# Ranks ahead of the last window groups, VectorE's tables spread over eight expert tiles, and twelve first sums ahead of the tail

## The reference

```python
x = x + gnn(layernorm(x))     # 3125 nodes x 256; 53125 edges, 8 edge types, summed at dst
h = layernorm(x)
probs = softmax(h @ gate_w + gate_b)         # 16 experts
top_probs, top_idx = top_k(probs, 2)         # weights normalised over the two
hidden = silu(h @ w1[e]) * (h @ w2[e])       # 256 -> 512
x = x + sum_k top_probs[k] * (hidden @ w3[top_idx[k]])   # 512 -> 256
```

## Time and profile before

| | |
|---|---|
| median of 3 runs | 917.49 us (916.19 to 918.03) |
| the profiled execution | 918.04 us |
| its span, first to last instruction | 916.3 us |
| TensorE matmuls | 738.9 us busy, 81% |
| TensorE weight loads | 627.0 us, 68% |
| VectorE | 517.8 us, 57% |
| GpSimd | 658.9 us, 72% |
| ScalarE | 301.6 us, 33% |

### The profile page before, as it was taken

One profiled execution on the slowest core, in us unless ns is written; L12 is line 12 of the kernel. 1 busy time (PEld: TensorE's weight loads), 2 busy tenths in 40 slices (PEclk: granted clock), 3 DMA queues, 4 the chain that ended last, 5 costly groups with the idle time before them and its releaser, 6 DMA issues.

```text
span 916.3 us, 18023 instructions
## 1 busy us (share of the span) xinstructions
PE 738.9 (81%) x4626; PEld 627.0 (68%) x4627; DVE 517.8 (57%) x1444; ACT 301.6 (33%) x469; POOL 658.9 (72%) x614
## 2 busy tenths in 40 slices
PE   0136887989788898888888888779999999999980
PEld 0124676877667776677767676558888888888870
DVE  6887646365464545647445577884444444344448
ACT  5524225222343323324233333122333333233323
POOL 7777777777777777777777750259798786987772
PEclk9997889899899999979999898999999999999995
DMA  9873445454455333343334324066656655663546
GB/s 204 252 227 98 145 145 181 133 161 145 145 150 157 106 104 106 104 131 103 106 104 133 103 82 166 24 234 232 217 189 217 224 182 174 222 212 97 160 137 182
DMA packets 91488, 141.92 MB, mean 155 GB/s; under 512 B 13197, under 2 KB 65889, under 8 KB 91456
## 3 DMA queue, kind: packets, MB, share of 16 engines
q0 software_dynamic: 25680, 70.16, 26.4%
q1 hardware_dynamic: 48854, 56.28, 19.3%
q10 hardware_dynamic: 16922, 15.15, 5.2%
HBM read 108.61 MB, written 32.93 MB: 154 GB/s over the span
## 4 chain that ended last, share of the span: by engine, by line
PE 43%; POOL 23%; issue 16%; DVE 9%; DMA 7%; ACT 1%; DVEq 1%; POOLq 0%; ACTq 0%; SPq 0%
POOL got L575 21%; PE ps L1710 16%; PE ps L1692 9%; PE ps L1549 7%; PE ps L1561 6%; DMA got<-x_tab,gidx 5%; PE ps L1718 3%; PE ps L1676 1%; PE ps L1645 1%; DVE ps L1474 1%; POOL part L581 1%; DVE stat L995 1%; DMA part<-in_x,early_idx 1%; DMA y_tab<-ffn 1%; POOL part L609 0%
## 5 line engine op out<-in xcount | busy, mean ns | idle before, releaser
L575 POOL DMA_INDIRECT got<-x_tab,gidx x388 | 370.3, 954 | 119.5 <-issue 112.7
L1549 PE MATMUL ps<-hot,got 125*128 125x256 f16 x1700 | 222.9, 293 | 75.6 <-DMA got<-x_tab,gidx 66.1
L1549 PEld LDWEIGHTS ps<-hot,got 125*128 125x128 f16 x1700 | 173.0, 104 | 121.0 <-DMA got<-x_tab,gidx 40.0
L1120 DVE TENSOR_TENSOR store<-store,ps 128x512 f32 x150 | 102.6, 684 | 182.1 <-PE ps L1549 151.0
L1561 PE MATMUL ps<-part,store 128*128 128x256 f32 x800 | 184.3, 389 | 0.5 <-DVE acc L1131 0.5
L1710 PE MATMUL ps<-part,operands 128*128 x696 | 177.9, 404 | 4.2 <-DVE operands L1396 3.1
L1561 PEld LDWEIGHTS ps<-part,store 128*128 128x128 f32 x800 | 154.5, 196 | 21.2 <-issue 0.5
L1710 PEld LDWEIGHTS ps<-part,operands 128*128 128x128 f32 x696 | 127.5, 190 | 31.5 <-issue 5.0
L1102 DVE TENSOR_SCALAR hot<-key_row,pass,drel 125x256 f16<-125x256 f16 x425 | 125.8, 363 | 12.4 <-issue 7.4
L1692 PE MATMUL ps<-part,operands 128*128 x696 | 98.3, 290 | 3.0 <-DVE operands L1406 2.6
L609 POOL TENSOR_TENSOR part<-store,part 128x2048 fp32r<-128x2048 f32 (+1 forms) x28 | 98.0, 3501 | 2.3
(11 more groups left out here) (252 smaller groups left out, 682.4 us busy)
## 6 DMA issues: line engine op xcount, KB each, us to landing
store<-in_L_ffn_w SPq DMA_DIRECT2D x48, 512.0 KB, 4.8
y_tab<-ffn SPq DMA_DIRECT2D x9, 896.0 KB, 4.6
y_tab<-ffn ACTq DMA_DIRECT2D x58, 128.0 KB
xs_tab<-x_sb SPq DMA_DIRECT2D x14, 512.0 KB, 3.1
ffn<-xs_tab ACTq DMA_DIRECT2D x55, 128.0 KB, 2.2
got<-x_tab,gidx POOLq DMA_INDIRECT x388, 2.7
acc<-in_x SPq DMA_DIRECT2D x5, 560.0 KB
x_tab<-got SPq DMA_DIRECT2D x5, 560.0 KB
```

Of the source, the lines that this page charges most:

```text
L575: nc.gpsimd.indirect_dma_start(got[:, c, :], None, x_tab, bass.IndirectOffsetOnAxis(ap=gidx[:, col:col + 1], axis=0)).then_inc(gathered[g] ...
L1120: v.tensor_tensor(window, window, ps[:, WIN_BANK[g], :].rearrange("p (q n) -> p q n", n=WIN), ALU.add).then_inc(win_added, 1)
L1549: last = mm(ps[:, WIN_BANK[g], k * KEYS:(k + 1) * KEYS], got[0:CE, c, a * DIM + k * P:a * DIM + (k + 1) * P], hot[0:CE, g % HOT, c - c0, : ...
```

## The change

Three edits. TensorE's `ranks` call, with its two waits, moves ahead of groups 3, 4 and 5 of the last tile. VectorE's tables are cut up and their order is changed: the rank sum and one product come before the first `low_xs`, `positions` comes before `order_tables`, `oct_tables` comes after tile 1, the splits of the first two experts are moved by a place, and `slots_needed` and `result_weights` are divided over tiles 3 to 7. In the tail a bank now takes two tiles in one copy of 512 columns, so that 12 tiles have room; six copies and eleven first additions are placed in and after the last two expert tiles, ahead of the last `copy_y`, and the twelfth behind it.

```diff
+        SUMS = 2 * len(SUM_BANK)
+        SOON_SUMS = 3
+        def sum_at(t):
+            n = t % SUMS
+            return ps[0:TP, SUM_BANK[n // 2], n % 2 * DIM:(n % 2 + 1) * DIM]
...
+            def keep_sums(q):
+                t0, t1 = 2 * q, min(2 * q + 2, TILES)
+                if t0 >= SUMS:
+                    act.wait_ge(out_ready, t0 - SUMS + 2)
+                bank = ps[0:TP, SUM_BANK[q % len(SUM_BANK)], 0:(t1 - t0) * DIM].rearrange("p (t d) -> p t d", d=DIM)
+                nc.scalar.copy(bank, acc[:, t0:t1, :]).then_inc(first_sum, 1)
...
-            for u in range(2):
-                expert_tile(early + (LAST_PAIRS - 1), u, load=False)
+            keep_sums(0)
+            keep_sums(1)
+            expert_tile(early + (LAST_PAIRS - 1), 0, load=False)
+            keep_sums(2)
+            expert_tile(early + (LAST_PAIRS - 1), 1, load=False)
             act.wait_ge(y_done, final_j + 1)
             high_hid(final_j)
             store_y(final_j - 1)
+            act.wait_ge(hid_ready, final_j + 1)
+            act.sem_inc(tiles_begun, 1)
+            act.wait_ge(xsT_ready, final_j + 2)
+            act.sem_inc(tiles_begun, 1)
+            for q in range(3, 6):
+                keep_sums(q)
             store_y(final_j)
...
             for t in range(TILES):
                 act.wait_ge(out_ready, t + 1)
-                if t + banks < TILES:
-                    keep_sum(t + banks)
+                if t % 2 and t - 1 + SUMS < TILES:
+                    keep_sums((t - 1 + SUMS) // 2)
                 act.dma_start(out[t * TP + p0:t * TP + p1, :], acc[p0:p1, t, :]).then_inc(out_stored, 16)
...
             final_j = dve.value_load(final[0:1, 0:1], min_val=0, max_val=SLOT_TILES - 1)
+            step(v.tensor_reduce(rank[:, :], smaller[0:1, :, :], AX.X, ALU.add))
+            offset_hots(hot1)
             low_xs(0)
+            offset_hots(hot2)
+            positions()
             order_tables()
-            positions()
-            split_first(0, (DOWN_PART,))
...
-            expert_tile(0, 0, first=True, tables=oct_tables)
-            split_first(1, (UP_PARTS, DOWN_PART))
-            expert_tile(0, 1, tables=slots_needed)
-            result_weights()
+            expert_tile(0, 0, first=True)
+            split_first(0, (DOWN_PART,))
+            expert_tile(0, 1, tables=lambda: split_first(1, (UP_PARTS, DOWN_PART)))
+            oct_tables()
             expert_tile(1, 0)
-            expert_tile(1, 1)
-            expert_tile(2, 0)
-            expert_tile(2, 1)
+            expert_tile(1, 1, tables=lambda: rows_upto(0))
+            expert_tile(2, 0, tables=lambda: rows_upto(1))
+            expert_tile(2, 1, tables=slots_needed)
+            expert_tile(3, 0, tables=result_weights)
+            expert_tile(3, 1, tables=sorted_weights)
...
+            for u in range(2):
+                expert_tile(early + (LAST_PAIRS - 1), u, firsts=range(u * SOON_SUMS, (u + 1) * SOON_SUMS))
...
             low_hid(final_j)
+            for t in range(2 * SOON_SUMS, SUMS - 1):
+                add_first(t)
             copy_y(final_j)
-            ahead = len(SUM_BANK) - 2
-            for t in range(ahead):
-                add_first(t)
+            add_first(SUMS - 1)
+            ahead = SUMS - 4
             for t in range(TILES):
-                if t + ahead < TILES:
+                if SUMS <= t + ahead < TILES:
                     add_first(t + ahead)
                 add_second(t)
...
                     t = TILES - 1
+                    pe.wait_ge(choice_step, (b * GEN_W + w) * SWEEP_STEPS + 2 * CHOICE_STEPS)
+                    pe.wait_ge(win_added, (v0 + TILES) * NG + RANK_BANK + 1)
+                    ranks(0, FIRST_PART).then_inc(ranks_begun, 1)
                     window(v0, t, 3)
                     window(v0, t, 4)
                     window(v0, t, 5, sweep, ODD)
-                    pe.wait_ge(choice_step, (b * GEN_W + w) * SWEEP_STEPS + 2 * CHOICE_STEPS)
-                    pe.wait_ge(win_added, (v0 + TILES) * NG + RANK_BANK + 1)
-                    ranks(0, FIRST_PART).then_inc(ranks_begun, 1)
                     turn_x2(v0 + t - 2)
```

More of the change, by code:

```diff
@@ L1355, in _, with offset_hots @@
             dve.wait_ge(owner_done, 3)
+            def offset_hots(hot_k):
+                step(v.tensor_tensor(hot_k, hot_k, bc(t_off[:, :], TE, 1), ALU.mult))
             def positions():
-                for hot_k in (hot1, hot2):
-                    step(v.tensor_tensor(hot_k, hot_k, bc(t_off[:, :], TE, 1), ALU.mult))
                 for k, hot_k in enumerate((hot1, hot2)):
@@ L1407, in low_hid, with expert_tile @@
                                 hidT[:, 0, :, :].bitcast(F32), ALU.subtract).then_inc(hidT_ready, 1)
-            def expert_tile(i, u, first=False, tables=None):
+            def expert_tile(i, u, first=False, firsts=(), tables=None):
                 j = i * 2 + u
@@ L1412, in expert_tile @@
                     low_hid(j - 1)
+                    for t in firsts:
+                        add_first(t)
                     if tables:
@@ L1425, in _, with rows_upto @@
             final_j = dve.value_load(final[0:1, 0:1], min_val=0, max_val=SLOT_TILES - 1)
-            pairs = dve.value_load(pairs_i[0:1, 0:1], min_val=EXPERTS // 2, max_val=SLOT_TILES // 2)
+            early = dve.value_load(early_i[0:1, 0:1], min_val=EXPERTS // 2 - LAST_PAIRS, max_val=SLOT_TILES // 2 - LAST_PAIRS)
+            step(v.tensor_reduce(rank[:, :], smaller[0:1, :, :], AX.X, ALU.add))
+            offset_hots(hot1)
             low_xs(0)
+            offset_hots(hot2)
+            positions()
             order_tables()
-            positions()
-            split_first(0, (DOWN_PART,))
+            def rows_upto(k):
+                dve.wait_ge(upto_kept, 2)
+                step(v.tensor_tensor(mine, upto_tile, bc(same[:, EXPERTS - 2 + k, :], [1, TILES, EXPERTS], 1), ALU.mult))
+                step(v.tensor_reduce(upto[:, k, :], mine, AX.X, ALU.add))
             def slots_needed():
[L1434 to L1438, removed]
                 step(v.tensor_scalar(upto_i[:, :, :], upto[:, :, :], float(P - 1), None, ALU.add))
@@ L1459, in result_weights @@
                 v.tensor_copy(pos2[0:TP, :, :], low_hi[:, :, :]).then_inc(pos2_done, 1)
-            expert_tile(0, 0, first=True, tables=oct_tables)
-            split_first(1, (UP_PARTS, DOWN_PART))
-            expert_tile(0, 1, tables=slots_needed)
-            result_weights()
+            expert_tile(0, 0, first=True)
+            split_first(0, (DOWN_PART,))
+            expert_tile(0, 1, tables=lambda: split_first(1, (UP_PARTS, DOWN_PART)))
+            oct_tables()
             expert_tile(1, 0)
-            expert_tile(1, 1)
-            expert_tile(2, 0)
-            expert_tile(2, 1)
+            expert_tile(1, 1, tables=lambda: rows_upto(0))
[3 more added lines that the diff above has]
+            expert_tile(3, 1, tables=sorted_weights)
             def add_first(t):
                 dve.wait_ge(y_got[t], 16)
[L1472 to L1477, removed]
+                dve.wait_ge(first_sum, t // 2 + 1)
+                v.scalar_tensor_tensor(out=sum_at(t), in0=y1[0:TP, t, :], scalar=wts2[:, 0, t:t + 1],
+                                       in1=sum_at(t), op0=ALU.mult, op1=ALU.add).then_inc(part_done, 1)
+            with dve.Fori(4, early + (LAST_PAIRS - 1)) as i:
                 for u in range(2):
                     expert_tile(i, u)
+            for u in range(2):
+                expert_tile(early + (LAST_PAIRS - 1), u, firsts=range(u * SOON_SUMS, (u + 1) * SOON_SUMS))
             def add_second(t):
```

14 lines of the change are left out of this document (3 added, 11 removed).

## The result

| | before | after |
|---|---|---|
| median | 917.49 us (916.19 to 919.60, 5 runs) | 921.72 us (920.29 to 925.78, 5 runs) |
| ratio | | 1.0059 [1.0038, 1.0080] |
| the profiled execution, its span | 918.04, 916.3 | 925.78, 924.1 |

The change made the kernel slower by 0.59%, about 5 us (3.5 to 7.3); 911.0 was forecast, with 908.4 to 913.8 as range.

What follows compares the result with a forecast made beforehand. No engine was taken to bound the whole (TensorE 43%), so each edit was priced in its own stretch: -1.85 + 0.4 - 5.5 = -6.95 from 918.04 gives 911.1, taken as 911.0 us; range 908.4 to 913.8.

Steps and rivals of the forecast that it cites:

- Edit 1: Last tile's window groups: ranks moved ahead of group 3 fill TensorE's idle time, hiding their whole 1.85 us; -1.85 us.
- The step in which groups 4 and 5 still start by their gather near 543.9: Ranks end at 541.75, group 3 starts 0.3 late and ends near 543.2, before the gather at 543.91.
- Edit 3: Tail: 12 first additions go ahead, 38 remain; VectorE ends 5.9 us earlier, SyncE's stores give back 0.4; -5.5 us.
- Edit 2: Tables, 590 to 630 us: VectorE gives back over 5 us, but tile 6 waits for GpSimd's weight split; +0.4 us.
- Each lies in the gap of 1.49 us in which VectorE waits for TensorE: nothing on the path: Tiles 3 to 7: table pieces of 1.2 us or under 1.5 us fit VectorE's wait for TensorE and cost nothing.
- the meeting: Tables: VectorE's split from 598.4 meets the fourth GpSimd gather with 1.95 us left, 0.6 more than before.
- First, ScalarE loads tile 4's rows in order: ScalarE's load stays at 607.86, so tile 1's down matmuls start at 610.3, tile 3 near 612.5, tile 6 ready near 627.2.
- rival D: Slower: new TensorE idle stretches lower the granted clock, which stays low; at 5 tiles the end is 921; chance 0.03.
- the gate: Start of tile 6, held by GpSimd's split of the third expert's weights; its end goes from 629.29 to 630.2.
- A: Tile 6's wait for GpSimd also shortens, the oct's stores landing 2 us sooner; tables give -2: 908.6; chance 0.12.
- B: Tail bound by DMA well below the burst rate: -4.2 or less instead of -5.5, 912.3 to 914; chance 0.12.

Runs made afterwards that it cites:

- e15_scalar_tiles: Kernel before plus surplus tensor_scalar operations of 1 x 50, five in tile 4 and five in tile 5: 925.05 us, ratio 1.0084.
- e16_reduce_tiles: Kernel before plus surplus tensor_reduce operations on 1 x 50, five in tile 4 and five in tile 5: 917.86 us, ratio 1.0003.
- e13_all_soon: Changed kernel with the tables of tiles 3 to 7 moved right behind oct_tables, ahead of GpSimd's first split: 912.53 us, ratio 0.9943 to the kernel before.
- e14_ranks_and_sums: Changed kernel without the tables' new order and places, keeping early ranks and early sums: 911.09 us, ratio 0.9927 to the kernel before.

## Why the prediction was wrong

**Edit 1 (-1.85): right in sign.** Measured -2.8 us, from -1.3 to -4.2. The step in which groups 4 and 5 still start by their gather near 543.9 did not hold. The ranks ended at 541.36, sooner than the forecast 541.75 although the choice was 1.70 late in this execution, but group 3 began only at 543.75, behind the stand of 2.39 us, and then ran 1.25 us longer at the lower clock. Neither was in the forecast, and VectorE's add for tile 23 came at 556.19, not near 553.6. From choice to transpose the stretch is 1.0 us shorter where 1.85 was forecast, and less than the median shows; where the rest of the 2.8 comes from isn't settled.

**Edit 3 (-5.5): right.** Alone it gave -5.1 (-3.4 to -6.8). VectorE's last result came 15.65 us after `copy_y`, forecast 15.2; SyncE's last issue 1.15 us behind it, forecast 1.5 (its last nine issues took 4.25 us, 0.47 each instead of 0.54). The two errors cancel: 5.36 less in this stretch.

**Edit 2 (+0.4): wrong by 11 us when alone, and the cause of the miss.** The step that failed is "Each lies in the gap of 1.49 us in which VectorE waits for TensorE: nothing on the path", with the pieces of tiles 5 to 7 "at an estimated 0.2 each". The 0.18 is true only while GpSimd runs no split. The rows for the right price were there: the earlier trace rows has a GpSimd subtraction of 4.61 us over tile 5. I used the meeting in one direction only, VectorE's long split that holds up a GpSimd gather, and never asked what GpSimd's split does to VectorE's short work. The pieces had been moved into tiles where GpSimd splits; before, the short ones ran from 606.7 to 611.8 us, while it stood idle (its last gather ended at 606.00, its index copy came at 611.95). `e15_scalar_tiles` shows the price without any other edit: +7.7 us; `e16_reduce_tiles`, 0.

The operations on VectorE that read a PSUM bank (`low_hid`, `hid`, `low_xs`, `copy_y`) took their usual 0.42 and 0.69 beside the same splits, which is why the trace of before gave no hint in its durations. The Trainium skill (SBUF — State Buffer, "Who interferes with whom") has this as a rule: a `tensor_scalar` in a 2-port mode, or a `tensor_tensor` with both inputs in SBUF beside a GpSimd operation that reads SBUF, excludes the other for the whole instruction, whoever issued first goes first, and a `tensor_reduce` never contends on trn2. The traces agree in all three: 3.70 and 4.36 us for a `tensor_scalar` of 0.18, 2.11 for the `tensor_tensor` L1476 (0.19 without a split), 0.18 to 0.19 for the reduction. In which mode a `tensor_scalar` ran, no row shows.

A second step failed beside it, in the paragraph that begins "First, ScalarE loads tile 4's rows in order": it kept the chain over this load at the times of before ("Nothing of that moves forward"), with tile 3 near 612.5 and tile 6 "ready near 627.2". `e13_all_soon`, which has no stand at tile 5, shows it best; its first index table is 1.52 us later than before, and its times here have that taken off. The forecast itself, further down, had SyncE's first store go 1 to 1.5 us later, but left ScalarE's load, `high_hid(1)` and TensorE behind it where they were. The store went 2.3 us later, the down matmuls of tile 1 began at 611.96 instead of 610.3, and the clock then fell to 0.50: rival D had that fall at 1.3 to 1.7 us and "covered by the wait for the gate"; it cost some 2.2 and was not covered. Tile 6 was ready at 631.07, 3.9 us later than forecast.

The gate was off in size only. The mechanism (the fourth gather stands behind VectorE's split, the first store goes later, and with it the index copy and GpSimd's split) was right: forecast +0.9 for the split's end, measured +2.15 after drift in the changed kernel and +1.75 in `e13_all_soon` (44.50 us behind the first index table against 42.75). So the two chains arrive together again, and later. Tile 6 starts there 1.56 us later against that table than in the trace of before (44.80 against 43.24); six traces with the old order of the tables, that one among them, have it between 42.81 and 44.56, so one trace would not show this by itself. The kernel is 1.4 us slower than `e14_ranks_and_sums` (912.53 against 911.09; the intervals overlap). Without the stand, then, edit 2 would have cost some 1.4 us at the medians, with 0 not excluded: near the upper bound of 1.5 that was given, and reached in part by another way. The whole forecast would have been missed by 1.5 us instead of 11.

Of the rivals, D had the right side and nearly the time (921), but not the cause. Both falls that it named came, the one before tile 3 (above) and one at tile 6. But the second came after a stop of 6.91 us, not instead of one, and cost 1.3 us in that tile's up matmuls, as D had priced it; the clock did not stay low for five tiles. A and B did not happen: the gate moved later, not sooner, and the tail kept its gain.

**Open.** The 2 us in which TensorE stands behind the ranks ahead of group 3, without a wait in the profile (1.85 to 2.39 in three kernels). In `e13_all_soon` it stands 1.91 us there, put down to VectorE's one-hot rows (`hot`, L1115), and the clock stays at 1.00; in the two traces of the slower chips it does not stand. The cause is not shown. The 1.25 us that after loses between tile 8 and the last tile are that execution's own, as far as one other trace can say: `e13_all_soon`, with all three edits, needs 250.5 us for this stretch, before 252.0.

## What to carry to other kernels

Before a small operation is moved to a gap on its engine, and the engine is VectorE, look at what GpSimd runs there: the price of the operation is not its duration but what is left of the other's instruction. It is paid again and again: of five operations in a row, three (`e15_scalar_tiles`) or four (the changed kernel) stood, and only those that fell between two GpSimd instructions passed. Such small VectorE work (`tensor_scalar`, `tensor_tensor` with both ends in SBUF) belongs ahead of GpSimd's long operations, or in a form that does not meet them. And a stand is to be read in both directions: a row in which GpSimd waits for VectorE is a reason to ask where VectorE will wait for GpSimd. Last, a transfer that is forecast to go later has to be followed to everything that waits for it, here to TensorE as well as to the gate.

## What the runs showed of the hardware that was not expected

A `tensor_scalar` on one row of 50 numbers, 0.18 us by itself, took up to 4.36 us beside a GpSimd subtraction of 4.5 us. In a row of five, those that stood ended one for one with GpSimd's operations (3.70, 0.98, 1.84 us beside operations that ended at 632.27, 633.27 and 637.83), and one between two of them took 0.24. GpSimd's own operations beside them took what they take elsewhere (4.60 us for 2048 columns, in the earlier trace rows 4.61), so the loss fell on VectorE alone.
